# The last image's short attention pass in front of its long one, and maxima sent six steps behind a pass, from two buffers

## The chip, the cores and the metric

The kernel runs on one core of one Trainium2 chip. The metric is the device time of the program in microseconds (us). The engines are named as the profile names them: PE is the tensor engine, DVE the vector engine, ACT the scalar engine, POOL the general-purpose engine (here it issues the gathers), SP the engine whose queue issues the other DMAs.

## The reference

Four images of 128 channels and 56 x 56 pixels go through two blocks. The first, a bottleneck with a deformable convolution:

```python
h = relu(bn1(conv1x1(x, w1)))                       # 128 -> 32 channels
off = conv3x3(h, woff) + boff                       # 27 channels: 9 taps x (dy, dx), 9 masks
samp = bilinear(h, y + dy, x + dx) * sigmoid(mask)  # 4 gathered corners for each tap
h = relu(bn2(einsum('bckhw,ock->bohw', samp, w2) + dcn_b))
x = relu(bn3(conv1x1(h, w3)) + x)
```

The second is a self-attention over the 3136 pixels of each image, with 16 channels for the queries, keys and values:

```python
f, g, h = wf @ x + bf, wg @ x + bg, wh @ x + bh
attn = softmax(einsum('bcq,bck->bqk', f, g), axis=-1)
x0 = einsum('bck,bqk->bcq', h, attn)
out = (wv @ x0 + bv) * gamma + x
```

## The kernel before

The 12544 pixels are cut into 28 chunks of 448 (7 for each image) and into 14 groups of 896. For each group POOL gathers, with one indirect DMA for each of the 9 taps of each of its 7 tiles of 128 pixels (line 477), the four corners from a table in HBM, 14 x 7 x 9 = 882 gathers, with a memset of a scratch tile `pad` between two of them (line 484). DVE multiplies and sums the corners (lines 1038 to 1052), PE turns them and applies w2 (lines 578 and 586), and then w3, the residual and the projections of the attention follow.

The attention of an image is cut into passes. A pass `(q, k0, k1)` takes the queries of chunk `q` against the keys of chunks `k0` to `k1`, in blocks of 112 keys or queries: 4 blocks for each chunk of keys. `STAGES` and `LAST_STAGES` (lines 87 to 91) list the passes in the order in which they run; with the last image there are 54 (numbers 0 to 53) of together 784 blocks. A pass does the following:

- "first logits" L1: for each block one matmul (line 602, into `L1a`, `L1b` and later `M`), and a maximum over it on DVE (line 1060).
- "maxima": DVE makes the running maximum and splits it into three bf16 rows in seven small operations (lines 1068 to 1084) that end in `MS`; PE turns `MS` with 4 small matmuls into the bank `A`, which is `L1c` (line 643), ACT copies the rows beneath the queries (line 825).
- "second logits" L2: for each block one matmul (line 619, into `L2a`, `L2b` and late in the kernel also `T`), then the exponential on ACT (line 812).
- "quad": for each four blocks, 4 matmuls with the values into `PV` (line 633).
- at the end of the pass ACT copies `PV` to `PVs` (line 820), PE turns and adds it ("sum", line 652, into `A`), DVE combines it with the chunk's earlier passes (lines 1103 to 1115). The last pass of a chunk goes on: reciprocal and product on DVE (lines 1119, 1124), "turn" on PE (line 662), copy on ACT (line 836), "value" on PE (line 669), and the result on DVE (line 1131). I call sum, turn and value together a pass's closing set. SP then stores the chunk (line 429).

The order on all engines comes from one plan, `plan(runs)`. It fills a list of steps ("ticks"); each holds at most one L1 block `x`, one L2 block `y`, one quad and one use of the bank `A`. A pass's maxima may be sent `CHAIN` steps behind its last L1 block, its first L2 block comes `READY` steps behind the maxima:

```python
if x == p.end:
    waiting.append((t + CHAIN, 0, p.index, "max"))
...
if t >= p.at.get("max", t) + READY and (y < ERING or len(quad_at) > (y - ERING) // 4):
    now["l2"] = y
```

The steps are laid over the groups: `QUOTA` and `LAST_QUOTA` say how many run within each half group, the rest behind the last gather's tile. Two uses of `A` are at least two steps apart. There is one buffer `MS`, so DVE's third small operation waits until PE has read the previous pass's maxima.

## Time and profile before

| | us |
|---|---|
| median of 3 timed runs | 1559.62 |
| the 3 runs | 1557.89, 1559.62, 1575.72 |
| the profiled execution | 1568.37 |
| its span (first to last instruction) | 1566.6 |
| PE matmul busy, 5781 instructions | 1190.6 (76%) |
| DVE busy, 2171 instructions | 968.9 (62%) |
| ACT busy, 1400 instructions | 681.5 (43%) |
| q0 (the gathers' queue), share of 16 DMA engines | 13.5% |

The span lies within the time of the profiled execution; 1.8 us lie around it. That execution was 8.75 us above the median of the timed ones. A row of the profile names the line of the kernel, the engine, the operation and the tiles, output first; a bracket at the end gives the idle time of that engine ahead of the row, and what released it. All four attention engines work in program order, each with its own list, and wait for each other on semaphores.

### The profile page before, as it was taken

How to read it: one execution, taken by the hardware profiler on the slowest of the kernel's cores; microseconds unless marked ns; L12 is line 12 of the kernel's file. 1: busy time of each engine (PE TensorE's matmuls, PEld its weight loads, DVE VectorE, ACT ScalarE, POOL GpSimd, SP SyncE). 2: the span in 40 equal slices, each digit the busy share in tenths (PEclk: the TensorE clock that was granted, in tenths of full speed). 3: DMA queues.
4: the chain of work that ended last, by engine and by line, in shares of the span. 5: the costliest groups of instructions: out<-in, count | busy, mean ns of one | idle time of the engine just before them, and what ended most of it. 6: DMA issues, size and time to landing. Idle time of an engine off the chain costs nothing.

```text
span 1566.6 us, 18944 instructions
## 1 busy us (share of the span) xinstructions
PE 1190.6 (76%) x5781; PEld 507.6 (32%) x5781; DVE 968.9 (62%) x2171; ACT 681.5 (43%) x1400; POOL 1215.9 (78%) x1673
## 2 busy tenths in 40 slices
PE   5617356388887877898588697898767877889997
PEld 2213122133433333343233242443223323333342
DVE  5444153387866764788466576767655865568781
ACT  2103022143654443465354444546344544457765
POOL 3788888888888888888888888888888888870000
PEclk9756758575978777688777776959577987799998
DMA  3231322211111111121111111121111111110000
GB/s 144 73 120 53 102 75 66 82 42 46 38 42 43 44 50 47 56 66 44 42 43 45 44 50 56 53 58 41 45 40 44 43 50 55 55 51 1 1 12 30
DMA packets 37325, 82.10 MB, mean 52 GB/s; under 512 B 15322, under 2 KB 17486, under 8 KB 36712
## 3 DMA queue, kind: packets, MB, share of 16 engines
q0 software_dynamic: 28224, 57.86, 13.5%
q1 hardware_dynamic: 8964, 22.93, 4.0%
q8 instruction: 47, 0.77, 0.2%
q14 instruction: 54, 0.44, 0.1%
q10 hardware_dynamic: 36, 0.10, 0.0%
HBM read 66.23 MB, written 14.59 MB: 52 GB/s over the span
## 4 chain that ended last, share of the span: by engine, by line
POOL 69%; PE 14%; issue 11%; DVE 5%; DMA 1%; another core or an unknown queue 0%; ACT 0%; POOLq 0%; DVEq 0%
POOL G L477 54%; POOL pad L484 15%; PE PV L633 3%; DVE mxp L1060 2%; PE L1a L602 1%; PE L1b L602 1%; PE L1c L652 1%; PE L1c L669 1%; PE L2a L619 1%; PE L2b L619 1%; DVE fold L1190 1%; DVE G L1038 0%; PE T L586 0%; PE L1c L662 0%
## 5 line engine op out<-in xcount | busy, mean ns | idle before, releaser
L477 POOL DMA_INDIRECT G<-table,IDX x882 | 946.6, 1073 | 187.9 <-issue 158.8
L1060 DVE TENSOR_REDUCE mxp<-L1b 112x1 f32<-112x448 f32 x378 | 234.3, 620 | 143.8 <-PE L1b L602 65.0
L812 ACT ACTIVATE H<-L2b 112x448 f32<-112x448 f32 x370 | 200.5, 542 | 280.1 <-PE L2b L619 187.0
L1060 DVE TENSOR_REDUCE mxp<-L1a 112x1 f32<-112x448 f32 x379 | 234.4, 618 | 69.8 <-PE L1a L602 32.5
L812 ACT ACTIVATE H<-L2a 112x448 f32<-112x448 f32 x370 | 200.1, 541 | 135.0 <-PE L2a L619 93.4
L484 POOL MEMSET pad<- 128x256 f32 x784 | 257.4, 328 | 0.5
L602 PE MATMUL L1b<-G,F 96*112 96x448 bf16 x378 | 174.0, 460 | 88.0 <-DVE mxp L1060 50.6
L633 PE MATMUL PV<-H,HT 112*17 112x448 f32 x1568 | 232.1, 671 | 0.9 <-ACT H L812 0.9
L602 PE MATMUL L1a<-G,F 96*112 96x448 bf16 x379 | 172.1, 454 | 68.9 <-DVE mxp L1060 54.7
L1038 DVE TENSOR_TENSOR G<-G,CW 128x640 f32<-128x640 f32 x196 | 145.8, 750 | 98.2 <-DMA G<-table,IDX 98.2
L619 PE MATMUL L2b<-F,G 99*112 99x448 bf16 x370 | 157.9, 427 | 2.4 <-issue 2.0
L619 PE MATMUL L2a<-F,G 99*112 99x448 bf16 x370 | 157.8, 427 | 2.3 <-issue 1.8
L602 PEld LDWEIGHTS L1b<-G,F 96*112 96x112 bf16 x378 | 55.7, 147 | 252.4 <-DVE mxp L1060 133.5
L586 PE MATMUL T<-ST,par 96*32 96x128 f32 x588 | 107.4, 333 | 8.8 <-ACT ST L798 7.2
L602 PEld LDWEIGHTS L1a<-G,F 96*112 96x112 bf16 x379 | 57.0, 150 | 162.4 <-DVE mxp L1060 80.2
L578 PE MATMUL T<-par,S 128*96 128x128 f32 x294 | 68.5, 357 | 33.2 <-DVE S L1052 23.8
L586 PEld LDWEIGHTS T<-ST,par 96*32 96x32 f32 x588 | 70.1, 132 | 60.1 <-issue 37.0
L798 ACT COPY ST<-T 96x384 f32<-96x384 f32 x98 | 46.3, 473 | 76.4 <-PE T L578 62.7
L803 ACT ACTIVATE h<-T,fold 32x128 f32<-32x128 f32 x98 | 43.9, 448 | 81.3 <-PE T L586 59.1
L1045 DVE TENSOR_TENSOR S<-G 128x576 f32<-128x576 f32 x98 | 73.5, 750 | 0.7
L652 PEld LDWEIGHTS L1c<-par,PVs 128*112 128x112 f32 x432 | 58.2, 210 | 35.3 <-issue 34.1
L619 PEld LDWEIGHTS L2a<-F,G 99*112 99x112 bf16 x370 | 58.0, 157 | 23.8 <-issue 14.8
(124 smaller groups left out, 1314.3 us busy)
## 6 DMA issues: line engine op xcount, KB each, us to landing
G<-table,IDX POOLq DMA_INDIRECT x882
table<-TS SPq DMA_DIRECT2D x24, 256.0 KB
out<-X SPq DMA_DIRECT2D x11, 448.0 KB
X<-xt SPq DMA_DIRECT2D x3, 1568.0 KB, 9.7
out<-X SPq DMA_DIRECT2D x6, 224.0 KB
offd<-OFS SPq DMA_DIRECT2D x28, 47.2 KB
OFG<-offd SPq DMA_DIRECT2D x13, 94.5 KB
X<-xt SPq DMA_DIRECT2D x1, 1120.0 KB, 6.5
```

What stands on the lines that cost most here:

```text
L477: eng.indirect_dma_start(G[:, j, k * 4 * CB:(k + 1) * 4 * CB], None, table[0:images * POS, :], bass.IndirectOffsetOnAxis(ap=IDX[:, g % IRI ...
L484: eng.memset(pad[:, :], 0.0).then_inc(s_pad, 1)
L578: mm = eng.transpose(T[0:96, t * 128:(t + 1) * 128], S[:, j % 2, t * 96:(t + 1) * 96], ident)
L586: mm = eng.matmul(O, P("w2", 96)[:, t * CB:(t + 1) * CB], ST[:, j % 2, t * 128:(t + 1) * 128], start=(t == 0), stop=(t == 2))
L602: eng.matmul(l1(x)[0:KT, 0:CHUNK], F6[0:STACK, p.chunk * CHUNK + qt * KT:p.chunk * CHUNK + (qt + 1) * KT], G6[0:STACK, p.image * PIX + kc ...
L619: eng.matmul(l2(y)[0:KT, 0:CHUNK], G6[0:STACK + 3, k:k + KT], F6[0:STACK + 3, p.chunk * CHUNK:(p.chunk + 1) * CHUNK], start=True, stop=Tru ...
L633: mm = eng.matmul(PV[32 * q:32 * q + CI + 1, 0:CHUNK], HT[:, key, :], E[:, y % ERING, :], start=(4 * w == p.block), stop=(4 * w + 4 == p.e ...
L652: mm = eng.matmul(A[0:KT, qt * (CI + 1):(qt + 1) * (CI + 1)], PVs[:, qt * KT:(qt + 1) * KT], P("sel"), start=True, stop=True)
L812: nc.scalar.activation(E[:, y % ERING, :], l2(y)[0:KT, 0:CHUNK], ACT.Exp).then_inc(s_exp, 1)
L1038: eng.tensor_tensor(rows, rows, weights.unsqueeze(2) .to_broadcast([128, n, CB]), ALU.mult).then_inc(s_mul, 1)
L1045: eng.tensor_tensor(S2[:, :, :], pair[:, :, 0, :], pair[:, :, 1, :], ALU.add)\
L1060: eng.tensor_reduce(mxp[:, p.q, qt, kc:kc + 1], l1(x)[0:KT, 0:CHUNK], AX.X, ALU.max)\
```

## The change

Three things change in the plan. The last two passes of the last image change places: the short one (5, 6, 7) of 4 blocks now runs ahead of (6, 0, 7) of 28 blocks, so that chunk 6 is finished last. `CHAIN` goes from 4 to 6. `MS` gets a second buffer, used by the passes in turn, and DVE waits for the read of the last pass but one. With these go a wait on ACT (its exponential of the rescaling factor waits until DVE has used the previous one of the same chunk of queries), and the stores of chunks 4 and 5 of the last image become one.

```diff
-               (5, 0, 6), (0, 5, 7), (1, 5, 7), (2, 4, 7), (3, 4, 7), (4, 5, 7), (6, 0, 7),
-               (5, 6, 7)]
+               (5, 0, 6), (0, 5, 7), (1, 5, 7), (2, 4, 7), (3, 4, 7), (4, 5, 7), (5, 6, 7),
+               (6, 0, 7)]
...
-CHAIN, READY, DRAIN, SUM = 4, 3, 3, 3
+CHAIN, READY, DRAIN, SUM = 6, 3, 3, 3
...
-        MS = sb("MS", [KT, 3, 4], BF16)
+        MS = sb("MS", [KT, 2, 3, 4], BF16)
...
-            store(b, 4, 5)
+            store(b, 4, 6)
             store(b, 6, 7)
-            store(b, 5, 6)
-            eng.wait_ge(s_out, 16 * (4 * IMAGES + 1))
+            eng.wait_ge(s_out, 16 * 4 * IMAGES)
...
                 eng.wait_ge(s_mc, p.maxops + 7)
+                before = [k for k in runs[:p.index] if k.q == p.q and not k.first]
+                if before:
+                    eng.wait_ge(s_cb, before[-1].combs + 1)
                 nc.scalar.activation(AL[:, p.q, :], DM[:, p.q, :], ACT.Exp).then_inc(s_al, 1)
...
-                    if p.index:
-                        eng.wait_ge(s_a, runs[p.index - 1].use["max"] + 1)
-                    ins = eng.tensor_copy(MS[:, 0, :], low)
+                    if p.index > 1:
+                        eng.wait_ge(s_a, runs[p.index - 2].use["max"] + 1)
+                    ins = eng.tensor_copy(part[:, 0, :], low)
```

The plan has 832 steps before and 833 after; the last L1 block stands in step 783 in both. In the changed kernel PE's lines have numbers smaller by one (601 for 602, 618 for 619, 632 for 633, 642 for 643, 651 for 652, 661 for 662, 668 for 669).

**PE, the maxima of pass 49, late in the kernel.** Before, from the pass's last L1 block (the first row) to its maxima (the last row):

```order
L602 MATMUL M<-G6,F6 112x448
L619 MATMUL L2b<-F6,G6 112x448
L602 MATMUL L1a<-G6,F6 112x448
L619 MATMUL T<-F6,G6 112x448
L633 MATMUL PV<-H4,HT 17x448 x4
L602 MATMUL L1b<-G6,F6 112x448
L619 MATMUL L2a<-F6,G6 112x448
L602 MATMUL M<-G6,F6 112x448
L619 MATMUL L2b<-F6,G6 112x448
L602 MATMUL L1a<-G6,F6 112x448
L619 MATMUL T<-F6,G6 112x448
L643 MATMUL L1c<-identb,MS 3x112 x4
```

Now the pass's last L1 block stands two L1 blocks ahead of the first row here; the piece ends with the maxima:

```order
L601 MATMUL L1b<-G6,F6 112x448
L618 MATMUL L2b<-F6,G6 112x448
L601 MATMUL M<-G6,F6 112x448
L618 MATMUL T<-F6,G6 112x448
L632 MATMUL PV<-H4,HT 17x448 x4
L601 MATMUL L1a<-G6,F6 112x448
L618 MATMUL L2a<-F6,G6 112x448
L601 MATMUL L1b<-G6,F6 112x448
L618 MATMUL L2b<-F6,G6 112x448
L601 MATMUL M<-G6,F6 112x448
L618 MATMUL T<-F6,G6 112x448
L642 MATMUL L1c<-identb,MS 3x112 x4
```

Between the pass's last L1 block and the line of its maxima there were 4 further L1 blocks and there are now 6; all of DVE's small operations keep their places behind the pass's last L1 block.

**PE, where the first logits end.** Before, from the last L1 block of the kernel (the first row):

```order
L602 MATMUL L1a<-G6,F6 112x448
L619 MATMUL T<-F6,G6 112x448
L643 MATMUL L1c<-identb,MS 3x112 x4
L619 MATMUL L2a<-F6,G6 112x448
L633 MATMUL PV<-H4,HT 17x448 x4
L619 MATMUL L2b<-F6,G6 112x448
L652 MATMUL L1c<-par,PVs 112x17 x4
L619 MATMUL T<-F6,G6 112x448
L619 MATMUL L2a<-F6,G6 112x448
L643 MATMUL L1c<-identb,MS 3x112 x4
L619 MATMUL L2b<-F6,G6 112x448
L633 MATMUL PV<-H4,HT 17x448 x4
```

After, from the same block:

```order
L601 MATMUL L1a<-G6,F6 112x448
L618 MATMUL L2a<-F6,G6 112x448
L618 MATMUL L2b<-F6,G6 112x448
L618 MATMUL T<-F6,G6 112x448
L618 MATMUL L2a<-F6,G6 112x448
L632 MATMUL PV<-H4,HT 17x448 x4
L651 MATMUL L1c<-par,PVs 112x17 x4
L618 MATMUL L2b<-F6,G6 112x448
L618 MATMUL T<-F6,G6 112x448
L661 MATMUL L1c<-par,NN 16x112 x4
L618 MATMUL L2a<-F6,G6 112x448
L618 MATMUL L2b<-F6,G6 112x448
```

Before, the maxima of both of the last passes (52 and 53) stood here, behind the last L1 block. Now only those of pass 53, the long one, do; they come two rows below the piece. Behind the last L1 block PE has 35 rows of second logits before and 37 after, and 10 quads in both.

**PE, the end of the program.** Before:

```order
L619 MATMUL T<-F6,G6 112x448
L633 MATMUL PV<-H4,HT 17x448 x4
L619 MATMUL L2a<-F6,G6 112x448
L633 MATMUL PV<-H4,HT 17x448 x4
L652 MATMUL L1c<-par,PVs 112x17 x4
L662 MATMUL L1c<-par,NN 16x112 x4
L669 MATMUL L1c<-XN,par 128x448
L652 MATMUL L1c<-par,PVs 112x17 x4
L662 MATMUL L1c<-par,NN 16x112 x4
L669 MATMUL L1c<-XN,par 128x448
```

After:

```order
L618 MATMUL T<-F6,G6 112x448
L618 MATMUL L2a<-F6,G6 112x448
L618 MATMUL L2b<-F6,G6 112x448
L618 MATMUL T<-F6,G6 112x448
L632 MATMUL PV<-H4,HT 17x448 x4
L618 MATMUL L2a<-F6,G6 112x448
L632 MATMUL PV<-H4,HT 17x448 x4
L651 MATMUL L1c<-par,PVs 112x17 x4
L661 MATMUL L1c<-par,NN 16x112 x4
L668 MATMUL L1c<-XN,par 128x448
```

Before, two closing sets stood behind the last second logits, those of passes 52 and 53; now only that of pass 53 does, and those of pass 52 stand between second logits further up. Of the stores, SP's last one is of one chunk (224 KB) in both.

## Rows read from the trace of the kernel before

**Rows 1.** Page, parts 1 and 2: busy time; 40 slices of POOL and granted clock

```profile
PE 1190.6 (76%) x5781; PEld 507.6 (32%) x5781; DVE 968.9 (62%) x2171; ACT 681.5 (43%) x1400; POOL 1215.9 (78%) x1673
...
POOL 3788888888888888888888888888888888870000
PEclk9756758575978777688777776959577987799998
```

**Rows 2.** Waits of POOL, whole span: waiter, releaser, us in total, times, longest

```profile
POOL G L477 <- issue: 158.8, 881, 0.3
POOL G L477 <- DVE MK L1016: 29.1, 1, 29.1
```

**Rows 3.** Timeline: start us, us, engine, line, operation, tiles, [idle before <-releaser]

```profile
1269.18 0.82 DVE L1038 TENSOR_TENSOR G<-G,CW 128x640 f32<-128x640 f32 x1 [5.48 <-DMA G<-table,IDX]
1403.92 0.95 POOL L477 DMA_INDIRECT G<-table,IDX  x1 [0.17 <-issue]
1420.25 0.82 DVE L1038 TENSOR_TENSOR G<-G,CW 128x640 f32<-128x640 f32 x1
```

**Rows 4.** Windows from 1270 us to the end of the span

```profile
core 0: us, PE busy (x) PEld busy (x) DVE busy (x) ACT busy (x) POOL busy (x), PEclk, DMA share, GB/s
1270.00:1410.00 140.00, 113.13 (x533) 48.75 (x533) 87.50 (x205) 65.18 (x135) 119.05 (x168) 0.79 0.18 52
1410.00:1524.60 114.60, 107.31 (x671) 45.58 (x670) 93.09 (x232) 80.00 (x171) 0.00 (x0) 0.99 0.01 5
1524.60:1549.90 25.30, 22.18 (x145) 8.05 (x143) 5.65 (x23) 19.61 (x42) 0.00 (x0) 1.00 0.08 29
1549.90:1566.60 16.70, 9.06 (x41) 4.36 (x37) 2.76 (x9) 2.59 (x6) 0.00 (x0) 0.64 0.08 28
```

**Rows 5.** Waits at PE's maxima: 1270 to 1410, then 1410 to the end

```profile
PE L1c L643 <- DVE MS L1080: 1.5, 2, 0.7
...
PE L1c L643 <- DVE MS L1082: 4.9, 9, 0.7
```

**Rows 6.** Timeline around one pass's maxima (columns as in rows 3)

```profile
1467.64 0.35 PE L619 MATMUL L2a<-F,G 99*112 99x448 bf16 x1
...
1468.42 0.15 DVE L1082 TENSOR_TENSOR MS<-res,MS 112x4 bf16<-112x4 f32 x1
...
1468.62 0.36 PE L643 MATMUL L1c<-identb,MS 112*3 112x112 bf16 x4 [0.63 <-DVE MS L1082]
```

**Rows 7.** Timeline of PE behind the last first logits: a maximum and quads

```profile
1529.47 0.36 PE L643 MATMUL L1c<-identb,MS 112*3 112x112 bf16 x4 [0.65 <-DVE MS L1082]
...
1533.80 0.94 PE L633 MATMUL PV<-H,HT 112*17 112x448 f32 x8
...
1540.09 0.94 PE L633 MATMUL PV<-H,HT 112*17 112x448 f32 x8
...
1544.56 0.95 PE L633 MATMUL PV<-H,HT 112*17 112x448 f32 x8
...
1546.79 0.95 PE L633 MATMUL PV<-H,HT 112*17 112x448 f32 x8
...
1549.02 0.95 PE L633 MATMUL PV<-H,HT 112*17 112x448 f32 x8
```

**Rows 8.** Timeline of PE, DVE and ACT at the end

```profile
1549.90 0.40 PE L619 MATMUL L2a<-F,G 99*112 99x448 bf16 x1
1550.04 0.53 ACT L820 COPY PVs<-PV 128x448 f32<-128x448 f32 x1
1551.16 0.95 PE L633 MATMUL PV<-H,HT 112*17 112x448 f32 x8 [0.86 <-ACT H L812]
1552.03 0.96 PE L652 MATMUL L1c<-par,PVs 128*112 128x17 f32 x8
...
1554.95 1.85 PE L669 MATMUL L1c<-XN,par 16*128 16x448 f32 x2 [0.61 <-ACT XN L836]
1556.84 0.68 DVE L1131 SCALAR_TENSOR_TENSOR X<-L1c,fold,X 128x448 f32<-128x448 f32 x1 [3.11 <-PE L1c L669]
1557.67 1.65 PE L652 MATMUL L1c<-par,PVs 128*112 128x17 f32 x8 [0.87 <-DVE X L1131]
1563.53 0.68 DVE L1131 SCALAR_TENSOR_TENSOR X<-L1c,fold,X 128x448 f32<-128x448 f32 x1 [3.48 <-PE L1c L669]
```

**Rows 9.** Timeline of PE: two neighbouring rows within 1270 to 1410

```profile
1350.96 0.91 PE L662 MATMUL L1c<-par,NN 112*16 112x112 f32 x4 [3.39 <-DVE ACC L1115]
1351.67 0.58 PE L602 MATMUL L1a<-G,F 96*112 96x448 bf16 x1
```

More of the change, by code:

```diff
@@ L642, in maxima @@
                 for qt in range(4):
-                    mm = eng.matmul(A[96:99, qt * KT:(qt + 1) * KT], MS[:, :, qt], identb[:, :],
+                    mm = eng.matmul(A[96:99, qt * KT:(qt + 1) * KT], MS[:, p.index % 2, :, qt], identb[:, :],
                                     start=True, stop=True)
@@ L1063, in maxima @@
             def maxima(p, k):
+                part = MS[:, p.index % 2, :, :]
                 low, old = NM[:, p.q, p.nth % 2, :], NM[:, p.q, 1 - p.nth % 2, :]
@@ L1073, in maxima @@
                 elif k == 2:
-                    if p.index:
-                        eng.wait_ge(s_a, runs[p.index - 1].use["max"] + 1)
-                    ins = eng.tensor_copy(MS[:, 0, :], low)
+                    if p.index > 1:
+                        eng.wait_ge(s_a, runs[p.index - 2].use["max"] + 1)
+                    ins = eng.tensor_copy(part[:, 0, :], low)
                 elif k == 3:
-                    ins = eng.tensor_tensor(res[:, :], low, MS[:, 0, :], ALU.subtract)
+                    ins = eng.tensor_tensor(res[:, :], low, part[:, 0, :], ALU.subtract)
                 elif k == 4:
-                    ins = eng.tensor_copy(MS[:, 1, :], res[:, :])
+                    ins = eng.tensor_copy(part[:, 1, :], res[:, :])
                 elif k == 5:
-                    ins = eng.tensor_tensor(MS[:, 2, :], res[:, :], MS[:, 1, :], ALU.subtract)
+                    ins = eng.tensor_tensor(part[:, 2, :], res[:, :], part[:, 1, :],
+                                            ALU.subtract)
                 elif k == 6:
```

## The prediction

> **What bounds the kernel now.** I read the page first. POOL is busy 78% of the span, at eight tenths or more in nearly every slice up to the 36th of 40, and then it is idle; the granted clock of PE wanders between 0.5 and 0.9 for all that time and is full only behind it [rows 1]. So there are two regimes: gathers up to about 1405 us, attention alone behind them. The list of waits says that POOL waits for another engine once only (29.1 us, near the start); the rest is 881 pauses of 0.18 us, its own issue [rows 2]. Nothing in the change touches POOL's list, and POOL is never held by the attention, so the gathers land when they do now.
>
> Where does attention begin to count? The timeline of DVE's products with gathered rows tells: the tile at 1269.18 us waited 5.48 us for its gathers, and it is the last that does. The last gather is issued at 1403.92, but its product starts only at 1420.25, 15.4 us after the issue ended [rows 3]. So up to 1269 every delay or gain of the attention engines is absorbed by waiting for gathers; from there to the end they set the time. Only these last 297 us can carry a change. The windows cut them in four [rows 4]: a stretch still mixed with tiles (140 us, clock 0.79), one with pairs of first and second logits (114.6 us, PE busy 107.3, DVE 93.1, ACT 80.0, clock 0.99: PE is nearest to its limit), one with second logits alone (25.3 us), and the end (16.7 us, PE busy 9.1: a chain of single steps).
>
> **The change, part by part.**
>
> *The end, the certain gain.* Now the last second logits start at 1549.90, and 16.70 us pass to the end of the span. Two closing sets lie in them, one behind the other, because both use the one bank: that of the long pass runs from its sum at 1552.03 to the end of its result at 1556.84 + 0.68 = 1557.52 (5.49 us), that of the short pass from 1557.67 to 1564.21 (6.54 us), and 2.39 us of store follow [rows 8]. Afterwards one set is left. From the last second logits: 1.26 us to the last quad (1549.90 to 1551.16), 0.95 for it, 0.07 to the copy (a quad at 1549.02 of 0.95, the copy at 1550.04) [rows 7, 8], 0.53 for the copy, some 0.06 to the sum; that makes 2.87. The set takes 5.49 (sum at the full rate) to 6.54 (all at half rate, the sum 1.65 us for 0.96); I take 5.8, since its sum comes 0.7 us behind a busy PE. With the store's 2.39 this is 11.06 us. **Term A: 11.06 - 16.70 = -5.6** (-5.9 to -4.9).
>
> *What moves ahead of the end.* The third closing set does not vanish, it goes between the second logits, and two steps more of delay leave two more of these behind the last first logits (37 rows for 35, 10 quads in both). The plain rhythm there is 2.23 us between quads (1544.56, 1546.79, 1549.02), so 0.56 us for a block; with a closing set in between, two quad intervals took 1540.09 - 1533.80 = 6.29 us instead of 4.46 [rows 7]. So the set costs 1.83 and the two blocks 1.12. One step also has no second logits (the long pass, whose maxima fall on the seventh step, starts a step late): 0 to 0.56, I take 0.3. **Term B: +3.2** (+2.9 to +3.6).
>
> *The maxima.* DVE's last small operation comes at 1468.42, and PE, through with its second logits of 1467.64, starts the four matmuls at 1468.62 after 0.63 us of idleness [rows 6]. Six steps behind, PE has two more pairs of logits to work on, and DVE's chain keeps its place, so this wait should be gone. Its total: 4.9 us in 9 waits behind 1410, and 1.5 us in 2 waits of 1270 to 1410 [rows 5]; two of the nine lie behind the last first logits, as the one of 0.65 at 1529.47 [rows 7]. Not all of it need come back, because PE then runs up against the banks of the first logits: DVE is at 93.1 of 114.6 us in the same stretch [rows 4]. The bounds are nothing and all; PE is the fuller engine, so I take three quarters behind 1410, and half ahead of it, where the clock and the tiles' work interfere. **Terms C: -3.7** (-4.9 to 0) **and D: -0.8** (-1.5 to 0).
>
> *At no cost:* the second buffer lets DVE write without waiting for the previous pass; without it DVE's third operation would hold the reductions queued behind it, and so PE's banks. ACT's new wait looks at an operation of DVE three steps or more back. If DVE were late there, ACT's exponentials behind it would wait; their cover is ACT's idle time, 34.6 of 114.6 us [rows 4]. The joined store of chunks 4 and 5 is issued well ahead of the last one, whose size and 2.39 us stay. SP's other stores come two steps later and nothing reads them.
>
> *Sum:* -5.6 + 3.2 - 3.7 - 0.8 = -6.9 us, with the terms' bounds from -9.4 to -1.3. The profiled execution is 1568.37 us, which gives 1561.5; it is 8.75 us above the median of the three timed runs, so I take the difference from the median: 1559.62 - 6.9 = **1552.7 us**.
>
> **The rivals.**
>
> *The wait only moves.* PE, freed at the maxima, waits for DVE's reductions at the next first logits. For it: DVE's seven small operations remain and delay the reductions. Against: DVE idles 21.5 us in that stretch [rows 4]. Terms C and D then are nothing: -2.4 us, 1557.2.
>
> *The clock rises.* PE's idle pauses and its clock go together here: 3.39 us of waiting at 1350.96, and the first logits behind it take 0.58 us, half rate, where logits of the same 448 columns take 0.35 at the full rate [rows 6, 9]. Fewer pauses could leave more of 1270 to 1410 at the full rate. PE is busy 113 of 140 us there; a granted clock of 0.85 for 0.79 makes that 113.1 x (1 - 0.79 / 0.85) = 8 us less, 1544.7 in all. Against it: the pauses taken away are of 0.7 us, and the long ones stay. The Trainium skill (TensorE: Matmul & The Clock Gate, in the part on HAM oscillation) says that pauses between bursts of matmuls send the array back to half rate; the row at 1350.96 agrees for a long pause, and no row here shows it for one of 0.7 us: seven of the nine short ones fall between 1410 and 1524.6, where the clock stays at 0.99. The sum above goes without that rule.
>
> *Slower: the clock falls* in the same stretch. Steps of the plan now meet the tiles' work elsewhere: sums, turns and maxima come two steps later beside the same products and projections, and a long wait like the one at 1350.96 can arise at another place, with some us at half rate behind it. From 0.79 to 0.71 costs 113.1 x (0.79 / 0.71 - 1) = 12.7 us: 1565.4. It decides from a clock of about 0.745, where it eats the whole gain (113.1 x (0.79 / 0.745 - 1) = 6.8). For it: in 40 slices the digits lie anywhere from 5 to 9 [rows 1]. Against: the change removes waits there and adds none.
>
> **How the numbers follow.** Forecast 0.55; the wait moves 0.17; the clock rises 0.13; it falls 0.13; something else 0.02. The forecast's own terms reach from 1550.2 to 1558.3, the clock cases from 1544.7 to 1565.4; the three timed runs of the kernel before lie from 1557.89 to 1575.72, so a median of a few runs can lie some us off by itself. I give 1543 to 1563 us. Faster or slower by over 2% (31 us, about what a measurement of this kernel can tell from no change) no case reaches: 0.03 for faster, 0.02 for slower, 0.95 within.
>
> **What would show it.** In the profile after: the last closing set alone behind the last quad, and some 11 us from the last second logits to the end; no wait for `MS` of 0.6 us at PE's maxima behind 1410; 37 second logits behind the last first ones in some 27 us; DVE's last wait for gathers near 1270 and the last gather near 1404 as now. Wrong it would be if PE's waits for DVE's reductions grew by what the maxima's lost, if the granted clock between 1270 and 1410 left 0.76 to 0.82, or if POOL began to wait for DVE.

## The result and the profile after

The changed kernel takes 1569.8 us (median of 20 runs, 1556.5 to 1575.7), the kernel before 1560.8 in the runs between them (20 runs, 1551.9 to 1575.7): ratio 1.005, 95% interval 1.003 to 1.007. The forecast was 1552.7, 6.9 us faster than before; it went the other way. The profiled execution after is 1570.85 us with a span of 1569.0 (before: 1568.37 and 1566.6). Medians are of all runs; a ratio leaves out the few executions that took over 1.5% longer than the fastest of their kernel, so that it can differ from the medians by some tenths of a per cent.

The page of after, as in [rows 1]; the second row is POOL and the third the granted clock in 40 slices:

```profile
PE 1196.5 (76%) x5781; PEld 523.8 (33%) x5781; DVE 962.8 (61%) x2171; ACT 682.4 (43%) x1400; POOL 1222.7 (78%) x1673
...
POOL 3888888888888888888888888888888888880000
PEclk9756657757687688776767788885577767787995
```

The work is the same: the counts agree to the instruction. The new thing is the right end of the third row. Before, it read 9998; now it reads 7995, and the last slice is at half rate nearly all through.

The windows of after behind the last gather, to be held against [rows 4] (columns as there; the last first logits start at 1519.90, the last second logits at 1556.50):

```profile
core 0: us, PE busy (x) PEld busy (x) DVE busy (x) ACT busy (x) POOL busy (x), PEclk, DMA share, GB/s
1413.00:1430.00 17.00, 15.70 (x57) 6.85 (x58) 10.61 (x30) 6.25 (x12) 0.00 (x0) 0.50 0.00 1
1430.00:1519.90 89.90, 87.26 (x557) 38.07 (x556) 74.45 (x190) 65.35 (x143) 0.00 (x0) 1.00 0.02 6
1519.90:1532.60 12.70, 11.17 (x76) 5.06 (x72) 4.01 (x17) 9.67 (x21) 0.00 (x0) 1.00 0.10 37
1532.60:1556.50 23.90, 23.90 (x84) 6.74 (x83) 2.13 (x6) 10.67 (x23) 0.00 (x0) 0.50 0.05 20
1556.50:1569.00 12.50, 6.78 (x27) 2.77 (x23) 1.32 (x4) 1.60 (x3) 0.00 (x0) 0.50 0.05 18
```

From these and [rows 3, 4] a ledger of the two profiled executions can be made, in us, by four marks: last gather issued, last first logits, last second logits, end.

| stretch | before | after | difference | forecast |
|---|---|---|---|---|
| start to last gather | 1403.9 | 1409.8 | +5.9 | 0 (D: -0.8) |
| last gather to last first logits | 120.7 | 110.1 | -10.6 | -2.7 (C, less what the next line has) |
| to last second logits | 25.3 | 36.6 | +11.3 | +2.2 (B, with C's -1.0 at the last two maxima) |
| to the end | 16.7 | 12.5 | -4.2 | -5.6 (A) |

The forecast's column adds up to its -6.9. The third line is what the forecast did not have. At 1532.60 the granted clock drops to half and stays there for the last 36.4 us. The first two lines are from executions that also differ in other ways (below), so they are not to be read one by one.

The timeline of PE in after, around that moment and further on (columns as in [rows 3]):

```profile
1528.17 0.95 PE L632 MATMUL PV<-H,HT 112*17 112x448 f32 x8
1529.04 0.96 PE L651 MATMUL L1c<-par,PVs 128*112 128x17 f32 x8
...
1530.79 0.55 PE L661 MATMUL L1c<-par,NN 112*16 112x112 f32 x4 [0.38 <-DVE NN L1128]
...
1531.96 1.29 PE L668 MATMUL L1c<-XN,par 16*128 16x448 f32 x2 [0.23 <-ACT XN L838]
1533.18 0.62 PE L618 MATMUL L2a<-F,G 99*112 99x448 bf16 x1
...
1548.02 1.70 PE L632 MATMUL PV<-H,HT 112*17 112x448 f32 x8
1551.45 1.70 PE L632 MATMUL PV<-H,HT 112*17 112x448 f32 x8
...
1556.51 0.62 PE L618 MATMUL L2a<-F,G 99*112 99x448 bf16 x1
1557.77 1.69 PE L632 MATMUL PV<-H,HT 112*17 112x448 f32 x8 [0.63 <-ACT H L811]
1560.12 1.68 PE L651 MATMUL L1c<-par,PVs 128*112 128x17 f32 x8 [0.65 <-ACT PVs L819]
1562.59 0.92 PE L661 MATMUL L1c<-par,NN 112*16 112x112 f32 x4 [0.79 <-DVE NN L1128]
1564.11 1.86 PE L668 MATMUL L1c<-XN,par 16*128 16x448 f32 x2 [0.61 <-ACT XN L838]
```

L651, L661 and L668 are a closing set: sum, turn, value. The clock falls as the value ends (1.29 us for what takes 1.01 at full rate), with pauses of only 0.38 us ahead of the turn and 0.23 us ahead of the value. A quad costs 1.70 us instead of 0.95, and quads come 1551.45 - 1548.02 = 3.43 us apart; the forecast's rhythm was 2.23 [rows 7].

The waits of after between 1410 and 1519.9 (waiter, releaser, total, times, longest), to be held against [rows 5]:

```profile
PE L1b L601 <- DVE mxp L1062: 2.7, 2, 2.5
...
PE L1a L601 <- DVE mxp L1062: 0.9, 2, 0.6
```

The waits for `MS` at the maxima are gone, as forecast; they came to 3.6 us in 7 waits in the same stretch of before. PE's waits for DVE's reductions are 3.6 us, where before had 2.2, and one of them is 2.5. Where that one comes from stands in two rows of after:

```profile
1412.27 0.82 DVE L1040 TENSOR_TENSOR G<-G,CW 128x640 f32<-128x640 f32 x1 [3.66 <-DMA G<-table,IDX]
...
1413.75 0.62 PE L601 MATMUL L1b<-G,F 96*112 96x448 bf16 x1 [2.50 <-DVE mxp L1062]
```

DVE waits for the last tile's gathers, which in before it never did behind 1269.18 [rows 3], and the 17 us at half rate from 1413 follow.

### The profile page after: what moved, and what is told of

It reads as the page before. It is cut to its first block, busy times and chain, and to the rows that moved or that the text cites. A ratio compares the mean times of both kernels' runs of the same rounds, so it can differ in the third digit from the quotient of the medians.

```text
span 1569.0 us, 18962 instructions
## 1 busy us (share of the span) xinstructions
PE 1196.5 (76%) x5781; PEld 523.8 (33%) x5781; DVE 962.8 (61%) x2171; ACT 682.4 (43%) x1400; POOL 1222.7 (78%) x1673
## 4 chain that ended last, share of the span: by engine, by line
POOL 75%; PE 10%; issue 10%; DVE 3%; DMA 1%; ACT 0%; POOLq 0%; DVEq 0%; ACTq 0%
POOL G L476 59%; POOL pad L483 16%; PE PV L632 3%; PE L2a L618 1%; PE L1b L601 1%; PE L1c L651 1%; PE L1a L601 1%; PE L2b L618 1%; DVE fold L1194 1%; PE L1c L668 1%; DVE mxp L1062 1%; PE T L618 1%; PE M L601 0%; DMA G<-table,IDX 0%; PE L1c L661 0%
## 5 line engine op out<-in xcount | busy, mean ns | idle before, releaser
L601 PE MATMUL L1a<-G,F 96*112 96x448 bf16 x379 | 177.2, 467 | 116.5 <-DVE mxp L1062 115.3
L632 PE MATMUL PV<-H,HT 112*17 112x448 f32 x1568 | 243.3, 701 | 0.6 <-ACT H L811 0.6
L618 PE MATMUL L2a<-F,G 99*112 99x448 bf16 x370 | 164.9, 446 | 0.6 <-ACT H L811 0.5
L618 PE MATMUL L2b<-F,G 99*112 99x448 bf16 x369 | 162.6, 441 | 1.0 <-ACT H L811 0.8
L802 ACT ACTIVATE h<-T,fold 32x128 f32<-32x128 f32 x98 | 43.9, 448 | 83.3 <-PE T L585 83.3
L577 PEld LDWEIGHTS T<-par,S 128*96 128x96 f32 x294 | 41.7, 165 | 110.3 <-issue 79.2
L651 PEld LDWEIGHTS L1c<-par,PVs 128*112 128x112 f32 x432 | 61.6, 220 | 39.9 <-issue 36.3
```

What stands on the lines that cost most here:

```text
L577: mm = eng.transpose(T[0:96, t * 128:(t + 1) * 128], S[:, j % 2, t * 96:(t + 1) * 96], ident)
L601: eng.matmul(l1(x)[0:KT, 0:CHUNK], F6[0:STACK, p.chunk * CHUNK + qt * KT:p.chunk * CHUNK + (qt + 1) * KT], G6[0:STACK, p.image * PIX + kc ...
L618: eng.matmul(l2(y)[0:KT, 0:CHUNK], G6[0:STACK + 3, k:k + KT], F6[0:STACK + 3, p.chunk * CHUNK:(p.chunk + 1) * CHUNK], start=True, stop=Tru ...
L632: mm = eng.matmul(PV[32 * q:32 * q + CI + 1, 0:CHUNK], HT[:, key, :], E[:, y % ERING, :], start=(4 * w == p.block), stop=(4 * w + 4 == p.e ...
L651: mm = eng.matmul(A[0:KT, qt * (CI + 1):(qt + 1) * (CI + 1)], PVs[:, qt * KT:(qt + 1) * KT], P("sel"), start=True, stop=True)
```

## The experiments

Times are medians; a ratio is to runs of the kernel before in between, on the same chip; brackets are 95% intervals. Where profiles are compared, "stretches" are the last three lines of the ledger: last gather to last first logits, to last second logits, to the end.

**First group: is the fall the cause, and which half of the change makes it?** Three runs with no new code: the changed kernel again; the order of the last two passes alone (with its stores); the maxima's delay and second buffer alone (old order and stores).

> The changed kernel once more, with a second profile. Theory K (the clock): in the profile of after the last first logits come 4.7 us sooner than before, but the granted clock is at half rate from 1532 us to the end, behind the long stretch with second logits and closing sets; this belongs to the new order, so the profile here shows a half-rate stretch of some 30 us or more at the end again, the stretch from the last first logits to the end takes some 49 us, and the time is 0.3 to 0.8% above before. Theory G (the gathers): the last gather was issued at 1409.8 instead of 1403.9; if the change makes the gathers slower, it is again 4 us or more later than in the other builds that have it, else it lies anywhere between 1402 and 1412.

Measured 1569.67 us, 1.0039 [1.0013, 1.0066], so the slowdown comes back in the times. But this time the profiled execution is one of the short ones, 1557.5 us, and its clock did not fall. Its windows from the last first logits:

```profile
1518.00:1545.20 27.20, 24.53 (x160) 9.51 (x156) 6.14 (x23) 20.32 (x43) 0.00 (x0) 1.00 0.09 35
1545.20:1555.70 10.50, 4.70 (x27) 1.88 (x23) 1.32 (x4) 1.64 (x4) 0.00 (x0) 0.76 0.06 22
```

27.2 + 10.5 us against 36.6 + 12.5 in the first profile of the same program: the fall costs 9.4 + 2.0 = 11.4 us. The twelve times lie in two bunches, three of 1555.3 to 1561.5 and nine of 1567.2 to 1574.6, their medians 13.1 us apart, and the mean granted clock of each execution parts them too: 0.744 to 0.748 in the three, 0.728 to 0.737 in the nine (36 us at half rate are 0.012 of 1560). So it looks as if the kernel has two ends, and the median falls into the dearer one. Other runs of the same kernel part less clearly (below).

```
-               (5, 0, 6), ..., (4, 5, 7), (6, 0, 7), (5, 6, 7)]
+               (5, 0, 6), ..., (4, 5, 7), (5, 6, 7), (6, 0, 7)]
```

> The kernel before with only the two last passes exchanged and the stores with them (CHAIN 4, one buffer). Theory K, if the third closing set among the second logits is what lets the clock fall: the end is at half rate here too, from about the third closing set on; the 5.6 us of the end are eaten by 7 us or more of half rate, and the time is 0 to 0.4% above before. Theory S (it is the sending at six steps that costs): no half-rate stretch but the last one, time 2 to 3 us (0.15 to 0.2%) below before.

Measured 1564.22, 1.0005 [0.9984, 1.0027]: no gain, though the end shrank to 10.8 us as the order promised. In its profile the clock is at half for 10.2 us from 1532.6, in the sum of the third closing set behind the last first logits. The rows of PE show the fall, and the windows behind them that the clock comes back at 1542.9, among second logits, without any extra matmul:

```profile
1529.60 1.01 PE L668 MATMUL L1c<-XN,par 16*128 16x448 f32 x2 [0.23 <-ACT XN L835]
...
1531.98 0.96 PE L651 MATMUL L1c<-par,PVs 128*112 128x17 f32 x8
1532.77 0.60 PE L618 MATMUL T<-F,G 99*112 99x448 bf16 x1
```

```profile
core 0: us, PE busy (x) PEld busy (x) DVE busy (x) ACT busy (x) POOL busy (x), PEclk, DMA share, GB/s
1532.60:1542.90 10.30, 10.30 (x35) 2.94 (x34) 1.31 (x4) 4.41 (x10) 0.00 (x0) 0.50 0.12 45
1542.90:1548.80 5.90, 5.39 (x35) 1.43 (x34) 0.00 (x0) 5.12 (x12) 0.00 (x0) 1.00 0.01 3
```

The maxima alone, in the changed kernel:

```
-               (5, 0, 6), ..., (4, 5, 7), (5, 6, 7), (6, 0, 7)]
+               (5, 0, 6), ..., (4, 5, 7), (6, 0, 7), (5, 6, 7)]
```

> The changed kernel with the old order of the last two passes (CHAIN 6, two buffers). Theory K: two closing sets among the second logits as before, the clock stays full until the last ones, the maxima's waits are gone, and the time is 2 to 5 us below before. Theory S: the time is 0.3 to 0.8% above before, as that of the changed kernel, because attention now runs up to the gathers, waits for them more often (259 us in all for 98) and has 837 us at half rate for 731. Theory G: its last gather is late, at 1408 or later.

Measured 1566.76, 1.0007 [0.9988, 1.0027]. The profiled execution fell too, at 1525.9 and to the end (stretches 114.8, 34.6, 18.6):

```profile
1524.22 1.01 PE L669 MATMUL L1c<-XN,par 16*128 16x448 f32 x2 [0.69 <-ACT XN L839]
1525.49 1.39 PE L633 MATMUL PV<-H,HT 112*17 112x448 f32 x8
1526.81 0.62 PE L619 MATMUL L2a<-F,G 99*112 99x448 bf16 x1
```

The fall comes in the quad behind the first set's value, and a full clock up to the last two sets had been expected. So each half alone can fall, both among the closing sets that share PE with second logits; neither half is "the" culprit. And three sets there are not needed: this kernel has two, like the one before.

**Keeping PE fed** (the last run of the first group). If the fall is the cause, matmuls of 448 columns (called wide here) put between the steps should take the loss away, although they are more work. They multiply loaded data into L1b, which nobody reads after the last reduction; the output is the same. Here 39 of them: one at every second step, one at each maximum, sum, turn and value among second logits, three ahead of the last quad and of each step of the last closing set, and three ahead of the first set's value, whose step has no second logits.

```
+            def idle(n):
+                for _ in range(n):
+                    eng.matmul(L1[1][0:KT, 0:CHUNK], F6[0:STACK, 0:KT],
+                               G6[0:STACK, 0:CHUNK], start=True, stop=True)
 ...
+                if t == only + 3:
+                    eng.wait_ge(s_red, len(owner))
+                if t >= only + 3:
+                    if now["l2"] is not None:
+                        idle((t % 2 == 0) + (now["use"] is not None))
+                    elif now["use"] or now["quad"] is not None:
+                        idle(3)
```

(`only` is the first step without first logits.)

> The changed kernel with extra matmuls of 448 columns into a bank that nobody reads, only behind the last first logits: one for every second step, one more at each use of bank A, three ahead of each step of the last closing set. It computes the same output. Theory K: the clock stays at full rate up to the end; of the 36.6 us from the last first to the last second logits some 27 to 28 are left, of the last 12.5 some 10.5 to 11, and the time is 8 to 11 us below that of the changed kernel, 1 to 3 us below before. If the half rate at the end is not the cause: as the changed kernel or up to 3 us slower, by the extra matmuls' own time.

Measured 1561.07, 0.9984 [0.9962, 1.0006]: 8.6 us below the changed kernel on the same chip. No half rate is left behind the last first logits (stretches 110.1, 30.0, 9.6), and the two bunches are gone: all twelve times lie in 1557.9 to 1566.8.

The second group asks whether such matmuls are simply good for any kernel, and where they act. The kernel before, as it is:

> The kernel before once more, for a second profile. In its first profile the last first logits came 120.7 us behind the last gather's issue; in the builds run since, 110 to 115 us, also in the one that changes only the order of the last two passes. If the first profile was one of the late ones, this one gives 110 to 116 us, and DVE's waits for gathers come to some 250 us as in all the others instead of 98. Theory K: the clock stays full up to the last two closing sets (2.2 us per quad), as in the first profile.

1567.67, 1.0009 [0.9979, 1.0039]. Its profile repeats the first one: stretches 119.9, 25.3, 16.7, no half rate in the middle one. (The 110 to 116 us and the 250 us of waits for gathers that I had expected were wrong: DVE waited 81.5 us.) The kernel before with the same 39 matmuls:

> The kernel before with the same extra matmuls behind its last first logits as in e4. Both kernels then have the full clock to the end, so e4 against this one is the change without the clock. If my sum was right but for the clock, this is 4 to 8 us slower than e4, at 1565 to 1569 us less what the full rate gives its last two closing sets (some 3 us): 1560 to 1566. If the change's own steps bring nothing, it equals e4's 1561 or is faster.

1566.83, 0.9997 [0.9971, 1.0024]: nothing, where 1560 to 1566 had been expected. The matmuls help only the kernel that falls. The changed kernel with the 24 beside second logits alone (without the `elif`), and then with the other 15 alone (`if now["l2"] is None and (...): idle(3)`), 12 at the end and the 3 ahead of the first set's value:

> The changed kernel with the extra matmuls only beside the second logits behind the last first ones, none in the last closing set. Theory K, as the profiles of after and e3 show it (the clock falls between the closing sets at 1526 to 1533 us): this alone keeps the clock until the last closing set, 1561 to 1563 us, 7 to 8 us below the changed kernel. Rival: the extra matmuls help only in the last closing set; then it is at 1568 or more.

> The changed kernel with the extra matmuls only ahead of the last quad and of the three steps of the last closing set. Theory K: the clock falls earlier, so this changes little: 1567 to 1571 us, and where the clock is at half rate the extra ones cost up to 2 us. Rival: 1561 to 1563.

The first: 1554.93 (8 runs), 0.9926 [0.9891, 0.9961], where 1561 to 1563 had been expected; the clock stays full to the last second logits (stretches 119.3, 29.8, 10.8). The second: 1562.13, 0.995 [0.992, 0.9981], on 9 runs from 1551.2 to 1576.5. Its profiled execution (1574.1 us) fell at 1536.4, right behind the second set's value, and the last 35.9 us are at half rate (last two stretches 36.0 and 13.9). Its median did better than expected of a kernel left to fall; its times reach over both bunches, so nine runs of it say little. What is shown is that feeding the end, and one step of the first set, doesn't keep the clock.

The third group splits the 24. The changed kernel once more and the 24 once more:

> The changed kernel again, to have it on the same chip as the next three and as the kernel before (chips differ: the mean granted clock of the kernel before was 0.740 on one and 0.753 on another). Theory K: its times fall into two bunches 10 to 14 us apart, by whether the clock falls between the closing sets; the median lies 0 to 9 us above before, depending on how many fall.

> The changed kernel with 24 extra matmuls of 448 columns beside the second logits behind the last first ones, as in e7. Theory K: 5 us or more below the changed kernel of this call and 2 to 11 us below before; the profile has the full clock from the last first to the last second logits, in 29 to 30 us.

1568.2, 1.0004 [0.9965, 1.0042], against 1560.2, 0.9949 [0.9917, 0.998]: 8 us apart on one chip. The windows from the last first logits of the first, then of the second:

```profile
1508.00:1517.90 9.90, 8.98 (x66) 4.05 (x62) 3.39 (x14) 7.17 (x15) 0.00 (x0) 1.00 0.05 21
1517.90:1545.70 27.80, 27.80 (x97) 8.41 (x96) 2.76 (x9) 13.29 (x28) 0.00 (x0) 0.50 0.07 27
```

```profile
1517.30:1547.10 29.80, 29.07 (x183) 12.59 (x180) 6.17 (x23) 20.70 (x43) 0.00 (x0) 1.00 0.08 32
1547.10:1557.90 10.80, 5.06 (x24) 1.86 (x22) 1.32 (x4) 1.60 (x3) 0.00 (x0) 0.66 0.06 21
```

37.7 us shrink to 29.8, though the records hold 183 matmuls for 163. (The first profiled execution still took only 1560.0, because its last gather was issued at 1390.2; the two other profiles of the changed kernel have it at 1407.9 and 1409.8. The start of the tail varies by itself.)

Then 16 matmuls at the closing sets and maxima only, and 8 in the plain rhythm behind the last closing set among second logits only:

```
+                    if now["l2"] is not None and now["use"]:
+                        idle(2)
```

> Of these 24 only the 16 at the steps of maxima, sums, turns and values, none in the plain rhythm of the last pass. Theory K with the closing sets as the cause: as e10 or up to 1 us faster. Rival (the whole stretch of second logits is too thin for the clock): in between e10 and the changed kernel.

```
+                    if now["l2"] is not None and t > max(p.at.get("value", 0) for p in runs[:-1]):
+                        idle(t % 2 == 0)
```

> Only 8 extra matmuls, in the plain rhythm behind the last closing set that stands among the second logits. Theory K with the closing sets as the cause: the clock has fallen before them, so nothing is kept, and the time is that of the changed kernel within 2 us (at half rate they cost up to 3 us, or they bring the clock back sooner). Rival: as e10.

At the sets: 1560.53, 0.9945 [0.9908, 0.9982]; stretches 115.3, 28.8, 10.8, clock full. In the plain rhythm: 1568.53, 0.9971 [0.9928, 1.0014], six times of 1550.4 to 1564.6 and six of 1572.5 to 1579.2. Its profile fell at 1533.9, in the second set's sum, and came back where its extra matmuls stand. They need not be the reason, since the order alone came back without any:

```profile
1524.30:1533.90 9.60, 8.68 (x63) 3.77 (x60) 3.35 (x14) 7.17 (x15) 0.00 (x0) 1.00 0.03 10
1533.90:1554.40 20.50, 20.50 (x69) 7.78 (x68) 2.76 (x9) 8.85 (x18) 0.00 (x0) 0.50 0.10 41
1554.40:1571.30 16.90, 11.02 (x61) 3.83 (x60) 1.31 (x4) 6.26 (x13) 0.00 (x0) 0.80 0.04 15
```

That places the loss: in every profile with a fall the clock goes at the closing sets among the second logits, and extra matmuls there keep it. The last closing set runs mostly at half rate too where no matmuls are added at the end, but so it does in the kernel before, and the forecast priced it.

**Fourth group: what the change is worth when the clock is kept.** With the matmuls at the sets and maxima everywhere, the fall is out of the comparison, and the forecast's terms can be measured one by one: the kernel before, order alone, maxima alone, both (12, 14, 14 and 16 extra matmuls by the condition above).

> The kernel before with two extra matmuls of 448 columns at each step of a closing set or maxima among the second logits behind the last first ones (12 in all). The clock stays full there before too in both profiles, so: as the kernel before, within 2 us. If it is 4 us or more below before, the clock fell in a share of the kernel before's executions as well, and my base was not free of it.

> The order of the last two passes alone (e2), with the same extra matmuls (14). By my sum -5.6 at the end and +1.8 for the set: 3 to 4 us below e13. Rival: the order alone brings nothing, within 1 us of e13.

> The sending at six steps and the two buffers alone (e3), with the same extra matmuls (14). By my sum -4.5 of waits at the maxima, +1.1 for two blocks, +0.3: 3 us below e13 (0 to 5). Rival: the waits only move to the banks of the first logits: 0 to 2 us above e13.

> The whole change with the same extra matmuls (16), as e11. By my sum 6.9 us below e13 (5 to 9). If the halves add up, it lies at e14 + e15 - e13.

| with matmuls at the sets | median us | ratio to before | stretches |
|---|---|---|---|
| before | 1563.51 | 1.0011 [0.9989, 1.0032] | 112.6, 26.4, 16.7 |
| order alone | 1558.28 | 0.9973 [0.9946, 1.0000] | 112.4, 28.0, 11.0 |
| maxima alone | 1562.41 | 1.0002 [0.9979, 1.0026] | 110.1, 26.2, 17.0 |
| both | 1559.47 | 0.9970 [0.9949, 0.9992] | 109.9, 28.8, 10.8 |

The windows of the first and of the last row:

```profile
1406.30:1519.00 112.70, 105.42 (x661) 45.27 (x660) 92.36 (x230) 79.22 (x170) 0.95 (x1) 1.00 0.02 6
1519.00:1545.30 26.30, 24.34 (x156) 9.50 (x154) 5.61 (x23) 19.77 (x42) 0.00 (x0) 1.00 0.07 28
1545.30:1562.00 16.70, 9.08 (x41) 4.36 (x37) 2.76 (x9) 2.62 (x6) 0.00 (x0) 0.64 0.08 28
```

```profile
1409.80:1519.80 110.00, 103.47 (x629) 45.42 (x628) 85.80 (x219) 73.21 (x158) 0.95 (x1) 0.94 0.02 6
1519.80:1548.50 28.70, 27.39 (x175) 11.45 (x171) 6.10 (x23) 20.59 (x43) 0.00 (x0) 1.00 0.09 33
1548.50:1559.40 10.90, 5.13 (x27) 2.00 (x23) 1.31 (x4) 1.69 (x4) 0.00 (x0) 0.69 0.06 21
```

The stretches sum to 155.7 against 149.5 us: -6.2, where the forecast has -6.9. By the ratios both together are -0.41%, some 6.4 us, by the medians 4.0. Order alone is -5.9 by the ratios (-5.2 by the medians, -4.3 in the profile), where -3 to -4 was expected. Maxima alone are -1.4, -1.1 and -2.4, where -3.1 was expected (-4.5 of waits, +1.4 for what moves behind the last first logits). In the times that can't be told from nothing.

**Fifth group: a better version.** Both parts, with matmuls at the sets and three ahead of each last step (31 in all):

```
+                    if now["l2"] is not None and now["use"]:
+                        idle(2)
+                    elif now["l2"] is None and (now["use"] or now["quad"] is not None):
+                        idle(3)
```

> The whole change with two extra matmuls at each step of a closing set or maxima among the second logits behind the last first ones (as e16), and three ahead of the last quad and of each step of the last closing set (31 in all). The last closing set then runs at the full rate: 9.6 us from the last second logits to the end for 10.8, so 5 to 7 us below the kernel before (e16 was 0.3% below).

1559.22, 0.9964 [0.9935, 0.9992]; stretches 110.1, 29.0, 9.6: the end is 1.2 us shorter than without the three. Its DVE waits 5.57 us for the last tile, and PE 4.74 behind it. And the same with more attention steps placed beside the last image's tiles:

```
-LAST_QUOTA = [24, 32, 36]
+LAST_QUOTA = [24, 32, 44]
```

> As e17, and the last half group takes 44 steps instead of 36 (LAST_QUOTA). If the wait for the last tile's gathers and the half rate behind it hold back the gain of the maxima: no wait of DVE for the last tile, no half-rate stretch of 14 us behind it, the last first logits 2 to 4 us nearer to the last gather, and 2 to 5 us below e17. If eight steps more ahead of the last tile only delay its work: the same as e17 or 1 to 3 us above.

1553.11, 0.9924 [0.9899, 0.995], faster than both kernels of this study. It was meant to take DVE's wait for the last tile away. It did not, though the wait is 2.96 us instead of 5.57:

```profile
1408.66 0.83 DVE L1055 TENSOR_TENSOR G<-G,CW 128x640 f32<-128x640 f32 x1 [2.96 <-DMA G<-table,IDX]
```

PE's longest wait behind it is 1.25 us instead of 4.74, and the half rate stayed, 13.6 us in two pieces (10.2 and 3.4) instead of 17.1. The stretch shrank to 105.7 from 110.1 us; 113 first and 149 second logits are left behind the last gather instead of 117 and 153. So the gain is measured (6.1 us against the run before it). How it divides between the shorter wait and the work done earlier, no run shows.

## Why the prediction was wrong

**Where the time goes.** POOL's list is unchanged and it never waits for attention; that held. "DVE's last wait for gathers near 1270" did not hold. In the first, fourth and fifth group of runs (all whose DVE waits for gathers sum to 244 us or more, below) each of the seven kernels with six steps' delay shows DVE waiting 2.9 to 5.6 us for the last tile at 1404 to 1417, as the profile of after does, and 13.7 to 27.3 us at half rate between the last gather and the last first logits; the three with four steps (order alone, and two with matmuls at the sets) show neither. With six steps the attention is further on when the last gather is issued: 117 first logits are left (113 with the longer quota), with four steps 126. But from that gather to the 100th last first logits it is 29.4 to 29.6 us in six of the seven profiles with 117 left (34.2 in the seventh, the maxima alone), and 29.3 in the three with 126. So the lead of nine blocks is used up there, where the wait and the half rate are. In the other two groups no kernel waits there, and 3.4 to 15.1 us are at half rate with either delay. This is read from profiles; no run takes the wait alone away.

**Term A, the end: right.** 11.06 us forecast; 10.5 to 11.0 in the six profiles whose clock held up to the last quad with nothing added behind it, 12.5 in the two of the changed kernel that fell. The saving of 5.6 came as 5.7 to 6.2 us.

**Term B, what moves ahead of the end: the step that failed.** It prices the third closing set and two blocks among second logits at the full-rate rhythm, +3.2 us, and B with the share of C is 2.2: 27.5 us for the stretch. Where the clock held it was 27.2. So the sum was right for the execution that the forecast imagined. What it lacked is that this stretch can lose the clock. The forecast did have a rival in which the clock falls, with the right sign and about the right price (12.7 us), but put it into 1270 to 1410, and of this stretch it wrote only of 37 second logits "in some 27 us", with the clock of 1.00 of [rows 4] taken for granted. The rule it cited was dismissed because pauses of 0.7 us left the clock at 0.99 in 1410 to 1524.6. That was a true reading of the kernel before, which held 1.00 even in the stretch with two closing sets; it says nothing of a stretch in which other work stands. With the fall priced at 11.4 us, -6.9 becomes +4.5; measured in three comparisons were +9.0, +6.8 and +1.6 us between medians (by the ratios +7.8, +6.1 and +0.6). So the fall gives the sign and most of the size; how the three come to differ is open.

**What is shown of the cause, and what isn't.** Shown: in all six profiles with a fall it starts among the closing sets beside second logits (at 1532.6, 1532.6, 1525.9, 1536.4, 1517.9 and 1533.9), also with either half of the change alone; 16 extra matmuls placed there remove both the fall and the loss, while 8 placed behind, or 12 at the end with 3 ahead of the first value, don't remove the fall; the same matmuls in the kernel before bring nothing. Of the seven profiles of kernels with the change or half of it that have no extra matmuls at the sets among second logits (or only ahead of one value) six fell; of the nine that have them there none did. Only argued: how often it falls. That some executions of the changed kernel fall and some don't is seen (two of its three profiles fell); that most do rests on the two bunches of times and mean clocks of one group of runs, and there is evidence against reading the bunches so. In the twenty runs of the first measurement an execution of 1556.5 us and one of 1568.9 have the same mean clock (0.739 and 0.740), the twelve of the third group do not part in two, and its profiled execution, with 40.3 us at half rate to the end, is the second shortest of them. The clock of the tail is known for profiled executions alone. Not settled: what decides it, and why the kernel before kept its clock there in both its profiles. It has two sets there for the changed kernel's three, with pauses of the same size (0.38 and 0.40 us) and two longer ones at the maxima (0.67 and 0.65); the kernel with the maxima alone has two sets as well and fell. Nor is it PE's share of busy time: 22.18 of 25.30 us in the kernel before, which kept the clock [rows 4], and 11.17 of 12.70 us ahead of the fall are both 88%.

The Trainium skill (TensorE: Matmul & The Clock Gate, HAM oscillation) tells of a clock lost to long waits between bursts of matmuls. The trace does not agree here as to the pauses: in the 12.70 us before the fall of after the longest is 0.38 us, and the longest ahead of any of the six falls is 0.69 (the maxima alone). The same page of the Trainium skill (A second HAM failure mode: psum-queue depth-cycling) has a clock that is lost to frequent small idle moments between groups of matmuls. Pauses of that kind are here, but they alone don't tell the kernels apart: before had eight in this stretch, together 3.1 us, and kept its clock, and after had five of together 1.5 us ahead of its fall. No run varied the pauses by themselves.

**Term C, the maxima behind the last gather: right.** The stretch from the last gather is a poor measure of it, because the kernels have different amounts of work left there. The last 100 first logits, all at the full rate, are a good one. They begin with the first row of each pair here and end with the second, in before and in after:

```profile
1441.25 0.40 PE L602 MATMUL L1a<-G,F 96*112 96x448 bf16 x1
1524.59 0.35 PE L602 MATMUL L1a<-G,F 96*112 96x448 bf16 x1
```

```profile
1439.36 0.35 PE L601 MATMUL L1a<-G,F 96*112 96x448 bf16 x1
1519.91 0.40 PE L601 MATMUL L1a<-G,F 96*112 96x448 bf16 x1
```

That is 83.34 us before and 80.55 after, 2.79 less. It repeats in every profile: 83.1 to 83.3 us in the six with four steps, 80.5 to 80.7 in thirteen with six (the fourteenth, with the longer quota, has tiles' work in it). PE's waits for `MS` there, 3.2 us, are gone, and its waits for DVE's reductions rise by only 0.3 us (0.27 to 0.56). So the rival "the wait only moves" is refuted there, and three quarters of the waits (2.4 us) was close, a little low. By these marks the execution of the changed kernel that kept its clock is 2.8 us shorter in the last 100 first logits, 1.9 longer up to the last second logits and 6.2 shorter at the end than before: 7.1 us less, with the fall of the other execution 4.4 us more.

**Term D, the maxima between 1270 and 1410: not measured.** What the delay wins ahead of the last tile may be the lead of nine blocks above, which is lost again in the same groups of runs; no run tells it from zero. The clock of 1270 to 1410, on which two rivals were built, lay between 0.71 and 0.82 in the 20 profiles, and between 0.74 and 0.79 in the three of the changed kernel alone.

**The base.** The two profiles of the start, before at a mean clock of 0.767 and after at 0.734, were no pair: the ledger's -10.6 repeats in no group of runs. There the stretch from the last gather to the last first logits is 112.5 against 110.1 us (order alone and the changed kernel, first group) and 112.6 against 109.9 (fourth; the extra matmuls all lie behind it). In the second group it is 119.9 and 115.0 with four steps, 119.3 and 123.2 with six, and tells nothing.

## What to carry to other kernels

Ask of every stretch that is to hold moved work whether TensorE's clock survives there, and price the move at both levels; a clock of 1.00 in the profile before belongs to the work that stood there then. Where a tail of single dependent steps is mixed with wide matmuls, a few wide matmuls without use at the dependent steps are a cheap test of that, and here were worth some 8 us of 1560. Measure a term over a fixed piece of work, between the same two matmuls in both kernels, and not from a mark that moves by itself, such as the last gather. And look at all the single times and at more than one profile: where an execution can end in two ways, a median says which way is more frequent, not what the change costs.

## What the runs showed of the hardware

- TensorE's clock fell to half with the engine busy for 88 to 91% of the 10 to 13 us before (11.17 of 12.70, 8.98 of 9.90 and 8.68 of 9.60 in three of the six profiles with a fall), and in three kernels stayed there to the end, for 35.9 to 44.1 us, although PE was then busy without a gap for most of it (23.90 of 23.90 us). In two others it came back among second logits: with the order alone after 10.2 us, with 8 extra matmuls in the plain rhythm after 20.5. I had expected a busy engine to keep or regain its clock. With the same share of busy time (22.18 of 25.30 us) the kernel before kept it.
- Extra work made a kernel faster: 16 to 39 matmuls of 448 columns, -7.7 to -8.6 us in the three comparisons with the changed kernel in the same group of runs, and nothing in the kernel before.
- One program's waits and clock differ more between groups of runs than any change of this study moves them. DVE's waits for gathers over the whole span sum to 71 to 120 us in the second and third group of runs and to 244 to 263 in the first, fourth and fifth, whatever the kernel, and the mean clock was about 0.753 in the former and 0.740 in the latter; the medians of the kernel before are 1566.6 and 1567.8 us in the former and 1561.2 to 1564.5 in the latter, so less waiting and a higher clock did not go with shorter times. It is not the chip: the second and the fourth group ran on the same one. The two profiles at the start are one of each kind:

```profile
DVE G L1040 <- DMA G<-table,IDX: 259.1, 55, 10.6
```

  in after, and `DVE G L1038` with 98.2 us in 22 waits in before.
